# Linear attention and expert gates on Trainium2: x loaded by feature, its moments spread through device memory, normalised on GpSimd

## The reference, cut to what matters

```python
def _layernorm(x, axis=-1, eps=1e-05):
    return (x - mean(x)) / sqrt(var(x) + eps)

n = _layernorm(x)
q, k = elu(n @ Wq.T + bq) + 1, elu(n @ Wk.T + bk) + 1      # 16 heads of 32
v = n @ Wv.T + bv
# causal, per head, along the sequence:
kv_t = kv_{t-1} + outer(k_t, v_t);  ksum_t = ksum_{t-1} + k_t
out_t = (q_t @ kv_t) / (q_t . ksum_t + 1e-6)
x = x + out @ Wo.T + bo
x = x + experts(_layernorm(x))      # top 2 of 8 by softmax; an expert that is
                                    # chosen by more tokens than its capacity is left out
```

## Time and profile before

| | |
|---|---|
| median of 3 runs | 2129.8 us (2128.57 to 2130.02) |
| the profiled execution | 2130.09 us, span 2128.4 us |
| TensorE busy | 2071.7 us, 97% |
| VectorE, ScalarE, GpSimd busy | 71%, 33%, 23% |
| mean granted clock of TensorE | 0.988 of 2.4 GHz |
| DMA | 110.43 MB, mean 52 GB/s |

### The profile page before, as it was taken

How to read it: one execution, slowest core, us unless ns; L and a number is a source line. 1 busy time by engine, 2 the same in 40 slices (tenths; PEclk the granted TensorE clock), 3 DMA queues, 4 the chain that set the end, 5 groups by cost and what they waited for, 6 DMA issues and landing times.

```text
span 2128.4 us, 61502 instructions
## 1 busy us (share of the span) xinstructions
PE 2071.7 (97%) x26420; PEld 1866.6 (88%) x26420; DVE 1504.4 (71%) x3193; ACT 703.5 (33%) x1415; POOL 494.3 (23%) x739
## 2 busy tenths in 40 slices
PE   6899999999999999999999999999999999999985
PEld 5799888999889999889999889899889999889884
DVE  4677767677766777767677767677767677667667
ACT  3333333333333333333333333333333333333321
POOL 3122222222222221222121222122222122222221
PEclk8999999999999999999999999999999999999997
DMA  4111111111111110111110111111111111111100
GB/s 154 36 51 40 53 51 60 53 51 37 55 51 56 56 51 33 60 51 56 56 51 31 61 51 51 61 51 31 61 51 51 61 51 32 57 55 51 41 32 31
DMA packets 60607, 110.43 MB, mean 52 GB/s; under 512 B 8368, under 2 KB 8368, under 8 KB 60336
## 3 DMA queue, kind: packets, MB, share of 16 engines
q1 hardware_dynamic: 57936, 105.93, 15.0%
q10 hardware_dynamic: 2400, 0.55, 0.1%
HBM read 72.90 MB, written 33.55 MB: 50 GB/s over the span
## 4 chain that ended last, share of the span: by engine, by line
PE 96%; DVE 2%; POOL 1%; issue 0%; DMA 0%; ACT 0%; SPq 0%; POOLq 0%; DVEq 0%
PE ring L551 35%; PE ring L537 33%; PE ring L601 7%; PE num_ps L635 5%; PE num_ps L623 5%; PE ring L612 3%; PE ring L525 3%; PE ring L574 2%; PE kv_ps L648 2%; PE ring L587 1%; POOL s_mask L381 0%; DVE s_mask L805 0%; DMA x_in<-in_x 0%; PE num_ps L331 0%; DVE stats L898 0%
## 5 line engine op out<-in xcount | busy, mean ns | idle before, releaser
L725 ACT ACTIVATE e_tmp<-ring,bias_n 128x512 f32<-128x512 f32 x256 | 175.9, 687 | 522.1 <-PE ring L537 522.1
L1075 POOL TENSOR_TENSOR k_sum<-k_sum,q_raw 128x512 f32<-128x512 f32 x128 | 167.3, 1307 | 727.5 <-DVE k_carry L828 727.5
L805 DVE TENSOR_TENSOR s_mask<-ring,causal 128x512 f32<-128x512 f32 x512 | 316.9, 681 | 0.5
L551 PE MATMUL ring<-wv_hi,xt_hi 128*128 128x260 f32 x1024 | 298.8, 292 | 1.9 <-DVE q_raw L816 1.9
L551 PE MATMUL ring<-wo_hi,o_hi 128*128 128x260 f32 x1024 | 295.5, 289 | 3.1 <-DVE o_lo L1011 3.1
L551 PE MATMUL ring<-wo_hi,o_lo 128*128 128x260 f32 x1024 | 291.5, 285 | 0.0
L551 PE MATMUL ring<-wv_hi,xt_lo 128*128 128x260 f32 x1024 | 290.2, 283 | 0.0
L551 PE MATMUL ring<-wo_lo,o_hi 128*128 128x260 f32 x1024 | 290.1, 283 | 0.0
L551 PE MATMUL ring<-wv_lo,xt_hi 128*128 128x260 f32 x1024 | 289.4, 283 | 0.0
L816 DVE SCALAR_TENSOR_TENSOR k_t<-ring,bias,e_tmp 128x512 f32<-128x512 f32 x128 | 96.1, 751 | 233.1 <-ACT e_tmp L727 231.0
L816 DVE SCALAR_TENSOR_TENSOR q_raw<-ring,bias,e_tmp 128x512 f32<-128x512 f32 x128 | 96.1, 751 | 177.4 <-ACT e_tmp L727 177.4
(11 more groups left out here) (134 smaller groups left out, 4025.5 us busy)
## 6 DMA issues: line engine op xcount, KB each, us to landing
x_in<-in_x SPq DMA_DIRECT2D x128, 256.0 KB, 3.7
res<-in_x SPq DMA_DIRECT2D x128, 256.0 KB, 2.7
out<-res SPq DMA_DIRECT2D x128, 256.0 KB, 2.0
q_raw<-in_wq_t SPq DMA_DIRECT2D x1, 1024.0 KB, 9.2
k_t<-in_wk_t SPq DMA_DIRECT2D x1, 1024.0 KB, 11.3
v_tok<-in_wv_t SPq DMA_DIRECT2D x1, 1024.0 KB, 13.5
k_t<-in_wo_t SPq DMA_DIRECT2D x1, 1024.0 KB, 15.4
q_div<-in_wo SPq DMA_DIRECT2D x1, 1024.0 KB, 14.9
```

The lines of the kernel that those rows point to most:

```text
L551: mm = pe.matmul(bank[:, 0:HW], rows[a](k), w[b][:, k, h, :], start=n == 0, stop=n == 3 * KD - 1)
L725: act.activation(e_tmp[:, m], bank, ACT.Relu, bias=bias_n[:, m, g:g + 1], scale=-1.0).then_inc(phi_relu.handle, 1)
L805: dve.tensor_tensor(s_mask[:, j], ring[:, BANK[u]].rearrange("p (g t) -> p g t", g=KD), repeat(causal, KD), ALU.mult).then_inc(free[BANK[u ...
L1075: pool.tensor_tensor(k_sum[:, g], k_sum[:, g], q_raw[:, g], ALU.mult).then_inc(prod.handle, 1)
```

## The change

x is also handed over transposed (x_t, features by tokens). SP loads each block twice: by token (x_tok, for mean and variance) and by feature (x_in, now features on partitions, tokens along the free dimension). The transposes on TensorE are gone. With tokens along the free dimension mean and reciprocal root are no longer a scalar per partition: they go as 4 KB to a buffer in device memory (moments_dram) and come back to all 128 partitions (x_rows, 128 x 1024 numbers; mean and root of tile c stand 8 numbers apart from token to token). GpSimd normalises with two instructions a tile (normalise), tiles 0 and 1 in front of the product of K3 at c = 2 and tiles 2 and 3 behind it. ScalarE and VectorE split from x_in instead of from the ring (split_x_high, split_x_low). The ring's list loses X and gets five places that nobody uses (SKIP). In the first step the weights' loads stand in front of spread_moments, and GpSimd normalises before it sets its constants.

```diff
-        uses += [("T", c)] + [("X", 0)] * last
-        uses += chunk_of(c, 0) + [("X", 1)] * last + [("R", g) for g in range(KD)] * last
-        uses += chunk_of(c, 1) + [("X", 2)] * last
-        uses += scores_of((c + 1) % TPB)
-        uses += chunk_of(c, 2) + [("X", 3)] * last + [("DEN", 0)] * (c == TPB - 2)
-        uses += [("O", (c, 0)), ("O", (c, 1))]
+        uses += [("T", c)] + chunk_of(c, 0)
+        uses += [("R", g) for g in range(KD)] * last + [("SKIP", TPB)] * last
+        uses += chunk_of(c, 1) + scores_of((c + 1) % TPB) + chunk_of(c, 2) + [("DEN", 0)] * (c == TPB - 2)
+        uses += [("O", (c, 0)), ("O", (c, 1)), ("SKIP", c)]
...
-assert len(USES) % NBANK == NBANK - 1
+assert len(USES) % NBANK == 0
...
+    x_feat = io["x_t"].rearrange("(k p) t -> p k t", p=P)
+    moments_dram = nc.dram_tensor("moments_rows", (2, P, TPB, 2), F32, kind="Internal").ap()
...
-    x_in = sb("x_in", [P, TPB, D])
+    x_tok = sb("x_tok", [P, TPB, D])
+    x_in = sb("x_in", [P, KD, BT])
+    x_rows = sb("x_rows", [P, P, TPB, 2])
...
         def load_x(st):
             a = st.off + 2
             if a > 0:
-                for k in banks_of("X"):
-                    sp.wait_ge(free[k].handle, free[k].at(st.before(k)))
-                    sp.sem_inc(waited[sp.engine].handle, 1)
+                sp.wait_ge(x_stat.handle, x_stat.at(TPB * a))
             for c in range(TPB):
-                sp.dma_start(x_in[:, c, :], x_t[st.lin(TPB, a, c), :, :]).then_inc(x_load[c].handle, 16)
+                sp.dma_start(x_tok[:, c, :], x_t[TPB * a + c, :, :]).then_inc(x_load[c].handle, 16)
+
+        def load_features(st):
+            a = st.off + 2
+            if a > 0:
+                sp.wait_ge(xt_lo.handle, xt_lo.at(TPB * a))
+            for k in range(KD):
+                sp.dma_start(x_in[:, k], x_feat[:, k, a * BT:(a + 1) * BT]).then_inc(xf_load.handle, 16)
+
+        def spread_moments(st):
+            a = st.off + 2
+            sp.wait_ge(x_rstd.handle, x_rstd.at(a + 1))
+            if a > 0:
+                sp.wait_ge(x_normed.handle, x_normed.at(TPB * a))
+            sp.dma_start(moments_dram[a % 2], mv0[:, a % 2]).then_inc(rows_out.handle, 16)
+            sp.wait_ge(rows_out.handle, rows_out.at(16 * (a + 1)))
+            rows = moments_dram[a % 2].rearrange("(o p) c s -> o (p c s)", o=1).to_broadcast([P, P * TPB * 2])
+            sp.dma_start(x_rows.rearrange("q p c s -> q (p c s)"), rows).then_inc(rows_load.handle, 16)
...
                 load_x(st)
+                load_features(st)
+                if not st.has("proj"):
+                    load_weights(sp)
+                spread_moments(st)
...
                 if c == 0 and st.has("turn"):
                     load_x(st)
+                    load_features(st)
+                if c == 2 and st.has("turn"):
+                    spread_moments(st)
...
-        run(sp, body, lambda: load_weights(sp))
+        run(sp, body)
...
-                        for k in banks_of("X"):
-                            pe.wait_ge(free[k].handle, free[k].at(st.before(k)))
+                        pe.wait_ge(xt_lo.handle, xt_lo.at(TPB * (st.off + 2)))
...
-        def turn_hi(st, c):
-            act.wait_ge(full[BANK[("X", c)]].handle, st.filled(("X", c)))
-            bank = ring[:, BANK[("X", c)]]
-            act.activation(xt[0][:, :, c * P:(c + 1) * P], bank.rearrange("p (k t) -> p k t", k=KD),
-                                       ACT.Copy).then_inc(xt_hi.handle, 1)
+        def split_x_high(st, c):
+            if st.has("proj"):
+                act.wait_ge(full[BANK[("V", (c, 1))]].handle, st.filled(("V", (c, 1))))
+            act.wait_ge(x_normed.handle, x_normed.at(TPB * (st.off + 2) + c + 1))
+            t = slice(c * P, (c + 1) * P)
+            act.activation(xt[0][:, :, t], x_in[:, :, t], ACT.Copy).then_inc(xt_hi.handle, 1)
...
-        def turn_lo(st, c):
-            u = ("X", c)
-            dve.wait_ge(full[BANK[u]].handle, st.filled(u))
-            bank = ring[:, BANK[u]].rearrange("p (k t) -> p k t", k=KD)
-            dve.wait_ge(xt_hi.handle, xt_hi.at(st.lin(TPB, st.off + 2, c + 1)))
+        def split_x_low(st, c):
+            dve.wait_ge(xt_hi.handle, xt_hi.at(TPB * (st.off + 2) + c + 1))
             t = slice(c * P, (c + 1) * P)
-            dve.tensor_tensor(xt[1][:, :, t], bank, xt[0].bitcast(F32)[:, :, t], ALU.subtract).then_inc(free[BANK[u]].handle, 1)
+            dve.tensor_tensor(xt[1][:, :, t], x_in[:, :, t], xt[0].bitcast(F32)[:, :, t], ALU.subtract
+                              ).then_inc(xt_lo.handle, 1)
...
-        def normalise(st, c):
-            a = st.off + 2
-            if c == 0:
-                dve.wait_ge(x_rstd.handle, x_rstd.at(st.lin(1, a, 1)))
-            dve.tensor_scalar(x_in[:, c], x_in[:, c], mv0[:, a % 2, c, 0:1],
-                                             rstd0[:, a % 2, c:c + 1], ALU.subtract, ALU.mult).then_inc(x_normed.handle, 1)
...
-            pool.tensor_tensor(rstd0[:, a % 2], var0[:, a % 2], neg_half, ALU.pow).then_inc(x_rstd.handle, 1)
+            pool.tensor_tensor(mv0[:, a % 2, :, 1], var0[:, a % 2], neg_half, ALU.pow).then_inc(x_rstd.handle, 1)
+
+        def normalise(st, c):
+            n = TPB * (st.off + 2) + c + 1
+            if c == 0:
+                pool.wait_ge(xf_load.handle, xf_load.at(16 * KD * (st.off + 3)))
+                pool.wait_ge(rows_load.handle, rows_load.at(16 * (st.off + 3)))
+            x = x_in[:, :, c * P:(c + 1) * P]
+            pool.tensor_tensor(x, x, repeat(x_rows[:, :, c, 0], KD), ALU.subtract).then_inc(x_centred.handle, 1)
+            pool.wait_ge(x_centred.handle, x_centred.at(n))
+            pool.tensor_tensor(x, x, repeat(x_rows[:, :, c, 1], KD), ALU.mult).then_inc(x_normed.handle, 1)
...
+                if c == 2 and turns:
+                    normalise(st, 0)
+                    normalise(st, 1)
                 if proj:
                     chunk(st, c, 1)
                 if proj:
                     chunk(st, c, 2)
+                if c == 2 and turns:
+                    normalise(st, 2)
+                    normalise(st, 3)
...
-    arrays = {"x": x.reshape(n_tok, D), "wq_t": np.asarray(L0_attn_Wq).T, "wk_t": np.asarray(L0_attn_Wk).T,
+    arrays = {"x": x.reshape(n_tok, D), "x_t": x.reshape(n_tok, D).T, "wq_t": np.asarray(L0_attn_Wq).T, "wk_t": np.asarray(L0_attn_Wk).T,
```

More of the change, by code:

```diff
@@ L80, in part_of @@
         return "proj" if place[0] == 0 else "attn"
-    return "attn" if kind in ("T", "O") else "turn" if kind == "X" else "proj"
+    return "attn" if kind in ("T", "O") else "proj"
 def uses_of(parts):
@@ L86, in uses_of @@
         return ring_uses_alone()
-    return [u for u in USES if part_of(*u) in parts]
+    return [u for u in USES if u[0] != "SKIP" and part_of(*u) in parts]
 def per_bank(parts):
@@ L211, in attention @@
     var0 = sb("var0", [P, 2, TPB])
-    rstd0 = sb("rstd0", [P, 2, TPB])
     std0 = sb("std0", [P, TPB])
@@ L393, in attention @@
     x_load = [sem(f"x_load{c}") for c in range(TPB)]
+    xf_load, rows_out, rows_load = sem("xf_load"), sem("rows_out"), sem("rows_load")
     res_load = [sem(f"res_load{n}") for n in range(2)]
     stored = [sem(f"stored{n}", 16) for n in range(2)]
-    x_stat, x_aggr, x_var, x_rstd, x_normed = (sem("x_stat"), sem("x_aggr"), sem("x_var"),
-                                               sem("x_rstd"), sem("x_normed"))
-    xt_hi, phi_relu, phi_exp = sem("xt_hi"), sem("phi_relu"), sem("phi_exp")
+    x_stat, x_aggr, x_var, x_rstd, x_centred, x_normed = (sem("x_stat"), sem("x_aggr"), sem("x_var"),
+                                                          sem("x_rstd"), sem("x_centred"), sem("x_normed"))
+    xt_hi, xt_lo, phi_relu, phi_exp = sem("xt_hi"), sem("xt_lo"), sem("phi_relu"), sem("phi_exp")
     k_scan, k_carried, prod = sem("k_scan"), sem("k_carried"), sem("prod")
@@ L412, in give @@
             eng.sem_inc(s.handle, s.credit)
-    loops = (n_blocks - 2) // 2
     base_m1 = per_bank(("turn",))
@@ L517, in _ @@
     def _(pe):
-        def turn(st, c):
-            u = ("X", c)
[L521 to L526, removed]
         def project(st, kind, g):
@@ L655, in body @@
             if not attn and not proj:
-                for c in range(TPB):
-                    turn(st, c)
                 return
@@ L662, in body @@
                     turn_keys(st, c)
-                if last and turns:
-                    turn(st, 0)
                 if c == 1 and not attn:
@@ L668, in body @@
                     if c == 0:
-                        for k in banks_of("X"):
-                            pe.wait_ge(free[k].handle, free[k].at(st.before(k)))
+                        pe.wait_ge(xt_lo.handle, xt_lo.at(TPB * (st.off + 2)))
                     chunk(st, c, 0)
-                if last and turns:
-                    turn(st, 1)
                 if last and proj:
@@ L677, in body @@
                     chunk(st, c, 1)
-                if last and turns:
```

(34 more changed lines are left out.)

1 line of the change is left out of this document (removed).

## The result

The changed kernel takes 2299.4 us (2292.3 to 2304.1, 4 runs) against 2129.9: a ratio of 1.079 (95% interval 1.0756 to 1.0824), slower by 7.9%. The forecast was 2240 us, with a range of 2150 to 2350. The profiled execution took 2304.1 us, span 2302.3.

What follows compares the result with a forecast made beforehand. TensorE, busy 97% of the span, was taken as the bound. 2130 - 54 (transposes) + 108 (stall) + 26 (clock) + 31 (start) = 2241, given as 2240 us; range 2150 to 2350.

Steps and rivals of the forecast that it cites:

- The bound and the mechanism: TensorE bounds the kernel; before the denominators it would wait for GpSimd's k_sum product, which had at most 0.3 us to spare.
- The stall: TensorE's wait before the denominators, behind two tiles' normalisation on GpSimd: 3.5 us in each of 31 blocks, 108 us.
- Saved on TensorE: Sixteen transposes a block gone, priced from denominators to the next step's first key transpose: 1.73 us, 54 us over 31 blocks.
- the scan's disturbance: VectorE's scan for K3 beside GpSimd's normalisation of tiles 0 and 1 adds up to 1.2 us.
- Rival A: GpSimd's strided read of x_rows makes each normalising instruction half dearer, 1.94 instead of 1.29 us: 2326 us; chance 0.27.
- The clock: TensorE at 1.2 GHz after the stall: half of the blocks lose 1.7 us, 26 us; bounds 0 and 105 us.
- The start: First step: moments' write behind the weights' loads, GpSimd's constants behind its normalisation; 31 us later, bounds 20 and 38.
- The sum: Time before, less saved transposes, plus stall, clock and start: 2241 us, given as 2240 us, slower by 5%.
- the second load of x: SP's load by feature, 256 KB x 4 more per block, hidden some 35 us ahead of its use: 0 us.
- the ring: Banks moved by five skips, TensorE waiting at none: 0 us, with 0.3 us a block (9 us) as the bad end.
- VectorE's split: The low split of x, reading SBUF instead of PSUM, keeps its length and isn't the bound: 0 us.

Runs made afterwards that it cites:

- product first: The changed kernel with all four normalisations behind the product of K3 instead of two in front of it: 2158.0 us, ratio 1.013.
- contiguous rows: The changed kernel with GpSimd reading the rows at one number a step, so other tokens' numbers; total 10308 us, only steady blocks compared: 66.85 us a block.
- moments before the store: The changed kernel with SP sending the moments in front of the store of tile 1 instead of behind it: 2219.6 us.
- one tile in front: The changed kernel with one tile's normalisation in front of the product of K3 instead of two, the others behind: 2198.1 us.

## Why the prediction was right, point by point

**The number**: the change was forecast to cost 110 us and cost 170. It is in the range, 59 us over the point forecast, and every term that costs time was forecast too low.

**The bound and the mechanism**: right. The stall is where it was forecast, in 31 blocks: TensorE waits for the product, and the product stands behind two tiles' normalisation in GpSimd's queue. With the product first the stall is gone.

**Saved on TensorE**: forecast 1.73 us a block, 54 us; measured 1.73. That both agree to the hundredth is luck. The forecast took one block, 22.12 us from D to T0, where the mean of 29 is 21.98, which would have given 1.59. A block is 64.1 us long, not the 66 that the prediction has; no term of the sum hangs on it.

**The stall**: forecast 3.5 us a block, 108 us; measured 133 (the waits' row, 4.3 us a block). By steps: the moments' write landed 1.8 us from issue (forecast 2.0), the rows 3.8 (forecast 3.35); four instructions and the scan took 7.1 us (forecast 6.6). What was mis-sized is mainly the instruction, 1.51 us for 1.29, four times, and next the rows' landing; the scan's disturbance was 0.9 us, not 1.2:

```profile
x_rows<-moments_rows SPq DMA_DIRECT2D x32, 512.0 KB, 3.8
...
moments_rows<-mv SPq DMA_DIRECT2D x32, 4.0 KB, 1.8
```

Rival A, the strided operand, was true in kind (18% dearer) and not in size (half dearer); its time, 2326 us, is 27 us over what was measured. Yet the stride is most of the miss: with contiguous rows the blocks are 56 us shorter in all, 35 by the stall and 20 by the clock.

**The clock**: forecast 26 us, measured 1.90 x 31 = 59. The step that took half of the blocks at 1.7 us was too low: all 30 blocks lose time, by 1.4 to 2.8 us. At stalls of 2.3 us (moments before the store) the clock costs 0.6 us a block, at 1.1 us 0.1.

**The start**: forecast 31 us. By the product-first run, which has no stall, the first denominators come 35.3 us late. The timeline shows the steps (forecast: the moments' write landed at 26, rows at 29.5, first projection at 46.6, constants' end at 57; the earlier trace rows has those of before). The prediction counted some 7 MB up to the last weight load of before; SP's loads there are 1 MB of x and 5 of weights, 6 MB. The landing that it worked out is right within 0.2 us all the same:

```profile
14.05 2.55 SPq L485 DMA_DIRECT2D moments_rows<-mv  x1
...
25.82 0.34 SPq L488 DMA_DIRECT2D x_rows<-moments_rows  x1
...
30.42 1.52 POOL L1068 TENSOR_TENSOR x_in<-x_in,x_rows 128x512 f32<-128x512 f32 x1 [20.14 <-DMA x_rows<-moments_rows]
...
48.17 0.77 PE L550 MATMUL ring<-xt_hi,wq_hi 128*128 128x512 f32 x1 [48.17 <-DVE wq_lo L291]
...
56.74 1.19 POOL L387 MEMSET order<- 128x1 f32 x8
```

**The sum** with measured terms: 2130 - 54 + 133 + 59 + 35 = 2303, against 2304 for the profiled execution. The terms are 62 us over those of the forecast: 33 in the clock, 25 in the stall, 4 in the start. The product-first run closes as well: 2130 - 54 + 35 + 49 = 2160, against 2159.

**Costed at 0**: the second load of x, the ring, and VectorE's split. The first two cost nothing that shows: GpSimd's 31 waits before it normalises all name the rows, and no steady stretch of TensorE is longer for the ring. The third was right for the changed kernel and wrong for any kernel without the stall. The split's two operands are now both in SBUF, so it waits for GpSimd when they meet; with the stall they don't meet, and without it that costs 49 us.

## What to carry to other kernels

Before work goes to an engine that is mostly idle, find what in its queue someone waits for and how much time that has to spare; here 0.3 us against 7 us of new work, with 77% of the engine free. Expect a short stall of TensorE to be paid again in clock, and a stall that is removed to uncover the next wait: price the fix by a run, not by the row of the wait. And when an operand of VectorE moves from PSUM to SBUF, look at what GpSimd reads from SBUF at that moment.

## What the runs showed of the hardware that was not expected

- A GpSimd tensor_tensor of 128x512 fp32 took 1.28 us with a contiguous second operand and 1.51 us with 32 bytes between its elements. The Trainium skill (GPSIMD Engine Reference, Performance pitfalls for Q7 kernels) gives +50% for such a read in kernels written for its cores; the built-in instruction paid 18%.
- The contention of GpSimd and VectorE goes both ways, and the one that starts second waits for the other's end. In the run with one tile in front, 62 of the 124 splits of the pipelined blocks started while a wide GpSimd instruction was under way. Each of them ended 0.55 us (0.545 to 0.554) behind that instruction's end, whether 0.4 or 1.6 us of it were left, and so took 0.95 to 2.2 us for 0.69. The scan does the same, 1.08 us behind the end. In the changed kernel GpSimd lost 0.9 us to a scan that started first (2.42 for 1.51), and that scan 0.15 (1.42 for 1.27) to the end of the GpSimd instruction before.
- VectorE's instructions with one operand in PSUM and one in SBUF took the same time beside GpSimd's wide instructions as alone: the divisions 0.67 and 0.68 us, the masking of the scores 0.68 both ways.
- A wait of TensorE of 4.1 us between dense work was followed by some 3.4 us at 1.2 GHz (granted clock 0.69 over 5.5 us), and 18 matmuls of 512 columns of no use in its place kept 2.4 GHz. Stalls of 2.0 to 2.8 us were followed by the low clock in some blocks and not in others (moments before the store).
